# Cross attention: minus the maxima written into the score banks by TensorE, and the probabilities weighed in three bf16 products

## The reference

```
q = rms_norm(x_normed @ Wq.T)            # 16 heads of 128, for 256 tokens
kv_in = concat([context (1601 rows), x_normed (256 rows)])
k, v = rms_norm(kv_in @ Wk.T), kv_in @ Wv.T   # 4 heads of 128
q, k = rope(q, positions), rope(k, positions)
probs = softmax(q @ k.T / sqrt(128))     # each k, v head serves 4 q heads
x = x + (probs @ v) @ Wo.T
```

## Time and profile before

| | |
|---|---|
| median of three runs | 1878.34 us (1871.86 to 1880.32) |
| the profiled execution's own time | 1877.92 us |
| its span, first to last instruction | 1876.0 us |
| mean granted clock of TensorE | 0.933 of 2.4 GHz |
| TensorE matmuls busy | 1583.5 us (84%), 8370 instructions |
| VectorE busy | 1397.3 us (74%) |
| GpSimd busy | 1149.8 us (61%) |
| ScalarE busy | 761.7 us (41%) |
| the stream's 480 steps | from 586 to 1762 us |
| DMA | 38 MB, 20 GB/s on average |

### The profile page before, as it was taken

How to read it: one execution, slowest core, us unless ns; L and a number is a source line. 1 busy time by engine, 2 the same in 40 slices (tenths; PEclk the granted TensorE clock), 3 DMA queues, 4 the chain that set the end, 5 groups by cost and what they waited for, 6 DMA issues and landing times. The chain is left out here.

```text
span 1876.0 us, 26248 instructions
## 1 busy us (share of the span) xinstructions
PE 1583.5 (84%) x8370; PEld 895.4 (48%) x8370; DVE 1397.3 (74%) x2946; ACT 761.7 (41%) x1802; POOL 1149.8 (61%) x987
## 2 busy tenths in 40 slices
PE   5586794644277999999899999999999999999787
PEld 4464473422133455455455455545545555554344
DVE  8686457667868788787977877878888787786455
ACT  2353554513433534344444443353434334433242
POOL 3652550130255779878678977777887767767442
PEclk8699897877679999999999999999999999999889
DMA  2000701000400000000000100000000000000010
GB/s 61 1 2 34 240 26 45 1 29 0 154 36 1 1 1 1 36 1 1 1 1 1 36 1 1 1 1 1 1 1 1 1 1 1 1 1 1 18 51 23
DMA packets 27855, 38.25 MB, mean 20 GB/s; under 512 B 4676, under 2 KB 24392, under 8 KB 27464
## 3 DMA queue, kind: packets, MB, share of 16 engines
q1 hardware_dynamic: 27720, 36.57, 5.8%
HBM read 35.51 MB, written 1.05 MB: 19 GB/s over the span
## 5 line engine op out<-in xcount | busy, mean ns | idle before, releaser
L1896 POOL TENSOR_TENSOR stream_acc<-stream_acc,stream_p 128x512 f32<-128x512 f32 x448 | 570.0, 1275 | 214.8 <-ACT stream_p L1819 210.3
L1819 ACT ACTIVATE stream_p<-stream_lowered 128x512 f32<-128x512 f32 (+1 forms) x480 | 302.4, 630 | 680.0 <-DVE stream_lowered L1956 678.7
L1761 PE MATMUL stream_banks<-stream_p,stream_v 128*128 128x512 f32 (+1 forms) x960 | 490.6, 593 | 0.9 <-ACT stream_p L1819 0.9
L1956 DVE TENSOR_TENSOR stream_lowered<-stream_banks,stream_shift_all 128x512 f32<-128x512 f32 (+1 forms) x480 | 329.8, 687 | 188.7 <-PE stream_banks L1748 162.6
L1963 DVE TENSOR_REDUCE stream_tops<-stream_banks 128x1 f32<-128x512 f32 (+1 forms) x512 | 322.8, 631 | 35.1 <-PE stream_banks L1734 35.0
L1734 PE MATMUL stream_banks<-stream_k_t_hi,stream_q_t_hi 128*128 128x512 bf16 (+1 forms) x512 | 186.2, 364 | 33.3 <-DVE stream_tops L1963 31.4
L1761 PEld LDWEIGHTS stream_banks<-stream_p,stream_v 128*128 128x128 f32 (+1 forms) x960 | 175.6, 190 | 57.8 <-ACT stream_p L1819 2.8
L1748 PE MATMUL stream_banks<-stream_q_t_hi,stream_k_t_hi 128*128 128x512 bf16 (+1 forms) x480 | 183.0, 381 | 0.0
L1748 PE MATMUL stream_banks<-stream_q_t_hi,stream_k_t_lo 128*128 128x512 bf16 (+1 forms) x480 | 182.1, 379 | 0.0
L1748 PE MATMUL stream_banks<-stream_q_t_lo,stream_k_t_hi 128*128 128x512 bf16 (+1 forms) x480 | 182.1, 379 | 0.0
L1901 POOL TENSOR_TENSOR stream_by_cos<-stream_by_cos,stream_by_sin 128x512 f32<-128x512 f32 x96 | 120.2, 1252 | 50.5 <-DVE stream_by_sin L1991 50.2
(11 more groups left out here) (398 smaller groups left out, 2972.0 us busy)
## 6 DMA issues: line engine op xcount, KB each, us to landing
memory_raw_t<-in_ctx_t SPq DMA_DIRECT2D x4, 1601.0 KB, 9.6
cross_ctx_t<-in_ctx_t SPq DMA_DIRECT2D x4, 1601.0 KB, 7.1
memory_raw<-in_ctx SPq DMA_DIRECT2D x4, 1536.0 KB
cross_w_raw_q<-in_L_xattn_Wq SPq DMA_DIRECT2D x1, 2048.0 KB, 11.9
cross_w_raw_o<-in_L_xattn_Wo SPq DMA_DIRECT2D x1, 2048.0 KB, 19.4
moe_raw_up<-in_L_ffn_wi SPq DMA_DIRECT2D x8, 256.0 KB, 4.3
model_x<-in_x SPq DMA_DIRECT2D x1, 1024.0 KB, 5.4
ffn_raw_fc<-in_L_ffn_w_fc SPq DMA_DIRECT2D x1, 1024.0 KB, 5.1
```

Of the source, the lines that this page charges most:

```text
L1761: nc.tensor.matmul(ps[:, 2 + n, :], v[0:r, g % 2, t, :], p32[0:r, step % 4, :], start=(t == 0), stop=(t == KT - 1)).then_inc(weighed, 1)
L1819: nc.scalar.activation(p32[0:r, step % 4, :], lowered[0:r, step % 3, :], ACT.Exp, scale=SCALE).then_inc(p32_ready, 1)
L1896: nc.gpsimd.tensor_tensor(acc[0:r, g % 2, cols], acc[0:r, g % 2, cols], p32[0:r, step % 4, :], ALU.add).then_inc(acc_ready, 1)
L1956: nc.vector.tensor_tensor(lowered[0:r, step % 3, :], ps[0:r, step % 2, :], shift_all[0:r, g % 2, n * HALF:(n + 1) * HALF], ALU.add).then_i ...
```

## The change

Minus the maxima no longer go through VectorE. Once for each pair of steps, ahead of the pair's scores, TensorE writes them into both score banks: for each bank one product of 32 rows, a constant 1/32 against 32 rows of `shift_all` (all equal), with rows 0 to 31 for bank 0 and 32 to 63 for bank 1, so that the two lie in different row tiles of the array. The scores are then added on top. `lower`, `lowered` and their semaphore go; ScalarE takes the exponential straight from PSUM.

The weighing is made of three bf16 products. The high words are not computed: the upper 16 bits of a float32 number are a bf16 number, and `upper` reads them in place, every other bf16 word. The low words of the probabilities are `p32` minus its upper half, a VectorE instruction for each step (`p_rest`, in the slot after); those of the values are a GpSimd instruction for each key tile (`values_rest`, slot 5 of a unit).

To go with that, `vary` leaves VectorE: the squares are scaled by 1/sqrt(128) as ScalarE takes them, and GpSimd adds 1e-6 in place ahead of the power (`root`, slot 6, ahead of `add_up`). The scaling itself leaves GpSimd for ScalarE, one activation a tile or head, in slot 8 (`normalise`).

```diff
+                def less_tops(step):
+                    g, j = divmod(step, STEPS)
+                    if j == 0:
+                        pe.wait_ge(side_taken, side_at[("spread", g, HALVES - 1)] + 1)
+                    if step >= HALVES:
+                        pe.wait_ge(p32_ready, step)
...
+                    for n in range(HALVES):
+                        rows = slice(32 * n, 32 * (n + 1))
+                        last = nc.tensor.matmul(ps[0:r, n, :], thirty[rows, 0:r], shift_all[rows, g % 2, n * HALF:(n + 1) * HALF],
+                                                start=True, stop=False)
+                    last.then_inc(seeded, 1)
...
-                    nc.tensor.matmul(ps[:, 2 + n, :], v[0:r, g % 2, t, :], p32[0:r, step % 4, :],
-                                     start=(t == 0), stop=(t == KT - 1)).then_inc(weighed, 1)
+                    p_hi, v_hi = upper(p32[0:r, step % 4, :]), upper(v[0:r, g % 2, t, :])
+                    nc.tensor.matmul(ps[:, 2 + n, :], v_hi, p_hi, start=(t == 0), stop=False)
+                    nc.tensor.matmul(ps[:, 2 + n, :], v_lo[0:r, g % 2, t, :], p_hi, start=False, stop=False)
+                    pe.wait_ge(p_lo_ready, step + 1)
+                    nc.tensor.matmul(ps[:, 2 + n, :], v_hi, p_lo[0:r, step % 3, :], start=False, stop=(t == KT - 1)).then_inc(weighed, 1)
...
                 for slot in SLOTS:
+                    if slot in range(0, ALL, HALVES):
+                        less_tops(slot)
                     if 0 <= slot < ALL:
                         score(slot)
...
-                    ac.wait_ge(lowered_ready, step + 1)
+                    ac.wait_ge(scored, step + 1)
...
-                    nc.scalar.activation(p32[0:r, step % 4, :], lowered[0:r, step % 3, :], ACT.Exp, scale=SCALE).then_inc(p32_ready, 1)
+                    nc.scalar.activation(p32[0:r, step % 4, :], ps[0:r, step % 2, :], ACT.Exp, scale=SCALE).then_inc(p32_ready, 1)
+
+                def normalise(u):
+                    ac.wait_ge(rms_ready, u + 1)
+                    ac.wait_ge(summed, u + 1)
...
+                    for h in range(width(u)):
+                        last = nc.scalar.activation(normed[:, h, :], by_cos[:, u % 2, h, :], ACT.Identity, scale=rms[:, u % 2, h:h + 1])
+                    last.then_inc(normed_ready, 1)
...
+                def root(u):
...
+                    nc.gpsimd.tensor_scalar(rms[:, u % 2, 0:n], ss[:, u % 2, 0:n], 1e-6, None, ALU.add).then_inc(mean_ready, 1)
+                    gp.wait_ge(mean_ready, u + 1)
+                    nc.gpsimd.tensor_tensor(rms[:, u % 2, 0:n], rms[:, u % 2, 0:n], half[:, 0:n], ALU.pow).then_inc(rms_ready, 1)
+
+                def values_rest(u, n):
...
+                    for t in tiles:
+                        last = nc.gpsimd.tensor_tensor(v_lo[:, g % 2, t, :], v[:, g % 2, t, :], upper(v[:, g % 2, t, :]), ALU.subtract)
...
-                def lower(step):
...
-                    nc.vector.tensor_tensor(lowered[0:r, step % 3, :], ps[0:r, step % 2, :], shift_all[0:r, g % 2, n * HALF:(n + 1) * HALF],
-                                            ALU.add).then_inc(lowered_ready, 1)
+                def p_rest(step):
+                    r = rows_of(step % STEPS // HALVES)
+                    ve.wait_ge(p32_ready, step + 1)
                     if step >= 3:
-                        ve.wait_ge(p32_ready, step - 2)
+                        ve.wait_ge(weighed, step - 2)
+                    nc.vector.tensor_tensor(p_lo[0:r, step % 3, :], p32[0:r, step % 4, :], upper(p32[0:r, step % 4, :]),
+                                            ALU.subtract).then_inc(p_lo_ready, 1)
...
-                    nc.vector.tensor_scalar(var[:, u % 2, 0:n], ss[:, u % 2, 0:n], 1.0 / HD, 1e-6, ALU.mult, ALU.add).then_inc(var_ready, 1)
```

More of the change, by code:

```diff
@@ L1658, in cross_stream, with upper @@
                     past[n] += step
+        def upper(ap):
+            return ap.bitcast(BF16).rearrange("p (n two) -> p n two", two=2)[:, :, 1]
         with nc.Block() as block:
@@ L1742, in score @@
                         pe.wait_ge(lo_ready, UNITS * (g + 1))
-                    if step >= 2:
-                        pe.wait_ge(lowered_ready, step - 1)
+                    for one, two in ((0, 0), (0, 1), (1, 0)):
+                        last = nc.tensor.matmul(ps[0:r, step % 2, :], k_t[one][:, g % 2, t * P:t * P + r], q_t[two][:, g % 3, 2 * n:2 * n + 2, :],
+                                                start=False, stop=(one == 1))
+                    last.then_inc(scored, 1)
+                def less_tops(step):
[4 more added lines that the diff above has]
+                        pe.wait_ge(p32_ready, step)
                     else:
                         pe.wait_ge(taken, early_taken)
[L1747 to L1750, removed]
+                        pe.wait_ge(thirty_ready, 1)
+                    r = rows_of(j // HALVES)
+                    for n in range(HALVES):
[3 more added lines that the diff above has]
+                    last.then_inc(seeded, 1)
                 def weigh(step):
@@ L1825, in square @@
                     if u >= 2:
-                        ac.wait_ge(var_ready, u - 1)
+                        ac.wait_ge(rms_ready, u - 1)
                     heads, some = projected_heads(u, n), part_tiles(u, n)
                     for h in range(some.start, some.stop):
-                        last = nc.scalar.activation(squares[:, h, :], heads[:, h - some.start, :], ACT.Square, accum_out=ss[:, u % 2, h:h + 1])
+                        last = nc.scalar.activation(squares[:, h, :], heads[:, h - some.start, :], ACT.Square, scale=SCALE,
+                                                    accum_out=ss[:, u % 2, h:h + 1])
                     last.then_inc(squared, 1)
@@ L1868, in _ @@
                             take_values(u, 1)
+                    for u in units_at(slot, 8):
+                        normalise(u)
                     for u in turns_in(slot):
@@ L1916, in _ @@
                         accumulate(slot)
+                    for u in units_at(slot, 5):
+                        if unit(u)[1] >= QT:
+                            values_rest(u, 0)
+                            values_rest(u, 1)
                     for u in units_at(slot, 6):
+                        root(u)
                         add_up(u)
-                    for u in units_at(slot, 7):
-                        normalise(u)
                     for b in range(1, BATCH):
@@ L2031, in _ @@
                 for slot in SLOTS:
-                    if 0 <= slot < ALL:
-                        lower(slot)
+                    if 0 <= slot - 1 < ALL:
+                        p_rest(slot - 1)
                     for item in pieces_in(slot):
@@ L2042, in _ @@
                         rotate(u, 0)
-                        if unit(u)[1] < QT:
-                            vary(u)
                     for u in units_at(slot, 6):
```

44 lines of the change are left out of this document (20 added, 24 removed).

## The result

The changed kernel takes 1945.23 us (median of 4, 1932.75 to 1946.63) against 1876.89 (4 runs, 1871.86 to 1880.32): ratio 1.035, 95% interval 1.0313 to 1.0387. It is slower by 66 to 68 us; 1944.0 was forecast.

A forecast was written before the change was run, and what follows sets the result against it. TensorE bounded the stream before; after, GpSimd was to bound three of six five-step periods: 3 x 12.8 + 3 x 12.3 + 2.3 = 77.6 us a group against 73.5, +66 over 16 groups on 1878.3, so 1944 (8 in 10: 1855 to 2000).

The forecast's parts named there:

- `p_rest`: VectorE, each step: 0.54 us plus the rest of GpSimd's instruction, taken as 1.04; +31.2 us a group.
- GpSimd held up: Each `p_rest` lengthens GpSimd's work by 0.43 us: +12.9 us a group where GpSimd has no slack.
- Weighing: TensorE: two fp32 instructions (0.85 us) become three bf16 ones (0.65), -6.1 us a group, strided reads at the packed rate.
- rival 3: Weighing on TensorE: strided reads run at the fp32 rate, +0.43 us a step, 2092 us in all; chance 0.06.
- Seeds: TensorE, each pair of steps: 0.22 us for overlapped products and 0.22 for tiling changes, 0.44 a pair, +6.6 a group.
- rival 4: TensorE: the two seeds of a pair run one after the other, 1966 us in all; chance 0.08.
- rival 5: ScalarE is held by GpSimd's late sums, 96 units x 0.5 us more, 1992 us in all; chance 0.09.
- The failed step: Slots ahead of the first step: GpSimd's changed instructions there cost 0, at most 5 us either way.
- Rival 1: Stream: `p_rest` falls into GpSimd's idle time, TensorE alone bounds; 1873, or 1820 with cheaper seeds, about 1850; chance 0.19.
- The sum by periods: Stream: work summed per five steps, three periods of 12.8 us and three of 12.3, plus 2.3, 77.6 a group.
- the 2.3 of coupling: Stream: queues holding each other up cost 2.3 us a group in the kernel before, assumed to stay.
- rival 2: Stream: load average, not periods, decides, 73.5 us a group again, 1878 us; chance 0.12.

The follow-up runs named there:

- one_input: Changed kernel with `p_rest` replaced by a VectorE maximum over the same 512 columns, one SBUF input, low words of the probabilities not computed: 1872.0 us.
- seed_full: Changed kernel with the seeds made by products of all 128 rows and a constant 1/128, without row tiles: 1941.9 us.
- scaling_split: Kernel before with only the `vary` and scaling moves, but the first nine units still scaled by GpSimd in slot 7: 1864.0 us.
- The mixes: Changed kernel with lowering back on VectorE, no seeds, two `normed` buffers, five or eight of 15 key tiles in three bf16 products: 1944.3 and 1936.1 us.
- mix_third: Changed kernel with lowering back on VectorE, no seeds, two `normed` buffers, five of 15 key tiles in three bf16 products: 1944.3 us.
- after_order: Changed kernel with `p_rest` moved from ahead of the pieces to the end of VectorE's slot: 1990.7 us.
- one_input_long: Changed kernel with `p_rest` replaced by a VectorE maximum over 960 columns, one SBUF input, low words of the probabilities not computed: 1906.7 us.

## Why the prediction was right, and where it was not

- **The forecast, 1944.0 against 1945.2**, was right in its mechanism. Part of the closeness is luck: the stream grew by 58 us where 66 were predicted, the lead by 11 where 0 was, and about 10 us of the stream's growth go with a lower clock (last section), for which the sum had no term.
- **`p_rest`**: 1.04 predicted, 1.08 measured (0.67 at best, 0.97 the median). The rows with GpSimd idle and one_input show the cause.
- **GpSimd held up**: 12.9 us a group predicted. Against one_input its additions, `v_lo`, 1e-6 additions and powers grew by 68, 29, 22 and 8 us in the stream, 7.9 a group, and all its instructions together by 9.0. The term was oversized by 4 us. With 0.30 instead of 0.43 for each `p_rest`, GpSimd's period comes out at 12.1 us and not 12.8 (an estimate), no longer than VectorE's 12.2: that GpSimd bounds three of the six periods is not shown. `v_lo` by itself is 0.41 (0.42 predicted), the addition of 1e-6 0.25 (0.22).
- **Weighing**: the strided high words cost 0.01 more than packed ones (0.227 and 0.225 us from start to start against 0.216); they do not take 0.43; rival 3 is out. TensorE's saving was thus about 0.19 a step, as in the sum.
- **Seeds**: 0.44 a pair predicted, 0.42 measured; rival 4 is out, and seed_full shows the tiling change to be as dear as the overlap is worth. What the sum left out is what the removed lowering gives back to TensorE by shorter waits: +63 us for the exchange, not +106.
- **ScalarE**: a scaling took 0.39 (0.29 start to start), not 0.27: laid together 117.5 us, +7.3 a group instead of 6.1. It did wait for sums (rival 5: 56.5 us), but TensorE waited only 13.4 us for the result.
- **The failed step: "in the slots ahead of the first step ... 0, at most 5 either way".** It was +11. I priced GpSimd's instructions there and left out that the scaling changes queues: on ScalarE the next unit's squares stand behind it, in a circle of 5.4 us. scaling_split puts it back and the lead is 70.2.
- **Rival 1 (the port has room)** needed a `p_rest` under 0.8. one_input, at 0.68, gives 1872: the rival's condition was right. So was its 1873 with the seeds at the price that the sum took; the 1850 mixed in a lower seed price that the trace does not bear out (0.42 a pair), and was 22 us too low.
- **The sum by periods** predicted 77.6 a group, and it is 77.0. That is nearer than its terms deserve: GpSimd's was too large, the clock's was missing, and the 2.3 of coupling was carried over from before. The mixes show why an average fails, which would have said no change (rival 2) here and 1852 for mix_third.

## What to carry to other kernels

Before moving work to VectorE, look at where its inputs lie: a 512-column instruction with two SBUF inputs beside a busy GpSimd cost 1.08 instead of 0.67 us and lengthened GpSimd's own by 13%, and that ate the whole gain of a faster product. When each slot needs two results of one engine, add its work up slot by slot, not over the group (after_order and the mixes suggest this; no run isolates it). A step that changes engines also changes what is queued behind it; check that in the filling phase, where there are no spare slots.

## What the runs showed of the hardware that was not expected

TensorE's clock left its upper level inside the stream. Its granted clock was 1.00 over the stream of before and 0.98 after, about 0.02 x 1232 / 0.5 = 49 us at the 1.2 GHz level (37 to 62 for the rounding); in one_input, one_input_long and seed_full it was 1.00. The windows of one place in the changed kernel: TensorE is idle for 0.67 us ahead of a piece at 947.36 and for 1.00 ahead of a transposition at 949.40, then runs at 0.50.

```profile
946.00:948.00 2.00, 1.33 (x7) 0.42 (x5) 2.00 (x4) 0.60 (x1) 0.66 (x2) 1.00 0.00 0
948.00:950.00 2.00, 1.00 (x7) 0.40 (x5) 2.00 (x6) 0.04 (x1) 0.68 (x1) 0.98 0.03 8
950.00:952.00 2.00, 2.00 (x6) 0.57 (x5) 1.05 (x2) 0.56 (x2) 0.00 (x0) 0.50 0.00 0
952.00:954.00 2.00, 2.00 (x8) 0.75 (x7) 1.70 (x3) 0.47 (x1) 1.26 (x1) 0.67 0.01 4
```

At the lower level a score starts 0.43 after the one before instead of 0.22, so 49 us there can hold up to 25 us of extra time. Two comparisons say how much of it counts. seed_full has the same `p_rest` (1.08 us in the mean) and additions (1.45) and a pair of seeds of the same price, at a clock of 1.00, and its stream is 9 us shorter (1222.9). And of the changed kernel's own four executions the three with a mean clock of 0.924 to 0.926 took 1944.3 to 1946.6 us, the one with 0.932 took 1932.8. So some 10 us of the 46 named above go with the clock; why it stays up in one execution and not in the next, these runs do not show.
